# Scores of two heads in the two halves of TensorE's rows, from fp32r high and low parts, in place of one head at a time from three bf16 parts

## The reference, cut to what matters

```python
q = (x @ Wq + bq).reshape(B, S, N_HEAD, HEAD_DIM).transpose(0, 2, 1, 3)
k = (x @ Wk + bk).reshape(B, S, N_HEAD, HEAD_DIM).transpose(0, 2, 1, 3)
...
scores = jnp.einsum('bhqd,bhkd->bhqk', q / math.sqrt(HEAD_DIM), k)
scores = scores + attention_bias
scores = jnp.where(src_mask, -jnp.inf, scores.astype(jnp.float32))
probs = jax.nn.softmax(scores, axis=-1).astype(v.dtype)
ctx = jnp.einsum('bhqk,bhkd->bhqd', probs, v)
```

## Time and profile before

| | before |
|---|---|
| median of three runs | 1060.0 us |
| the profiled execution | 1060.6 us, of which the span of the instructions 1058.7 us |
| PE busy (whole span) | 1006.1 us, 95% |
| DVE, ACT, POOL busy | 840.7 us (79%), 790.2 us (75%), 634.2 us (60%) |
| bytes moved by DMA | 269 MB |

### The profile page before, as it was taken

One profiled execution on the slowest core, in us unless ns is written; L12 is line 12 of the kernel. 1 busy time (PEld: TensorE's weight loads), 2 busy tenths in 40 slices (PEclk: granted clock), 3 DMA queues, 4 the chain that ended last, 5 costly groups with the idle time before them and its releaser, 6 DMA issues.

```text
span 1058.7 us, 19427 instructions
## 1 busy us (share of the span) xinstructions
PE 1006.1 (95%) x6870; PEld 758.3 (72%) x6936; DVE 840.7 (79%) x1966; ACT 790.2 (75%) x1291; POOL 634.2 (60%) x333
## 2 busy tenths in 40 slices
PE   5999999999799999999999999999999799999998
PEld 4789988888565655656666665666666589999997
DVE  6599999998868988989889898998988555555553
ACT  6755577555599899999999999999999344444443
POOL 3565766664246877798787997878877332222110
PEclk9999999999899999999999999999999999999999
DMA  8746788759799999998999989999895131111001
GB/s 234 263 146 222 247 295 301 276 180 378 304 330 398 409 373 358 352 340 322 367 355 340 357 322 362 345 347 343 313 338 199 40 120 60 60 61 40 21 20 40
DMA packets 103249, 269.44 MB, mean 254 GB/s; under 512 B 7522, under 2 KB 63586, under 8 KB 86642
## 3 DMA queue, kind: packets, MB, share of 16 engines
q1 hardware_dynamic: 103154, 268.21, 70.5%
HBM read 217.57 MB, written 50.61 MB: 253 GB/s over the span
## 4 chain that ended last, share of the span: by engine, by line
PE 49%; DVE 12%; DMA 12%; POOL 10%; ACT 8%; issue 7%; SPq 2%; DVEq 0%; ACTq 0%; POOLq 0%
PE psH L540 11%; DMA t_bt<-in_fside_Bx16xSxS 10%; PE psO L540 10%; PE psT L650 9%; POOL t_bt L1423 8%; PE psQ L540 5%; PE psV L663 5%; PE psS L639 4%; ACT t_bt L894 3%; DVE t_x L1026 2%; SPq L255 2%; PE psA L540 2%; ACT t_pt L780 2%; DVE t_bt L1215 2%; PE psX L692 1%
## 5 line engine op out<-in xcount | busy, mean ns | idle before, releaser
L1423 POOL TENSOR_TENSOR t_bt<-t_bt,t_mb 128x1024 f32<-128x1024 f32 x182 | 384.6, 2147 | 89.0 <-DMA t_bt<-in_fside_Bx16xSxS 88.8
L1215 DVE CUSTOM_DVE_ANT_0 t_bt<-psS,t_bt 128x512 f32<-128x512 f32 x512 | 338.2, 684 | 61.1 <-PE psS L639 39.6
L894 ACT ACTIVATE t_bt<-t_bt,t_nm 128x512 f32<-128x512 f32 x512 | 356.6, 732 | 20.4 <-DVE t_nm L1215 20.3
L650 PE MATMUL psT<-t_idf,t_bt 128*128 128x128 f32 x2048 | 308.6, 274 | 5.2 <-issue 2.5
L650 PEld LDWEIGHTS psT<-t_idf,t_bt 128*128 128x128 f32 x2048 | 252.9, 141 | 66.0 <-ACT t_bt L894 12.7
L780 ACT ACTIVATE t_pt<-psT 128x512 f32<-128x512 f32 x317 | 191.2, 603 | 18.9 <-PE psT L650 18.2
L639 PE MATMUL psS<-t_ks,t_qs 128*128 128x512 bf16 x482 | 183.9, 382 | 8.0 <-DVE t_nm L1215 3.7
L1225 DVE COPY t_pt<-psT 128x512 f32<-128x512 f32 x195 | 133.8, 686 | 1.7 <-PE psT L650 1.7
L663 PE MATMUL psV<-t_pt,t_vs 128*17 128x512 f32 x1024 | 134.2, 598 | 0.0
L639 PEld LDWEIGHTS psS<-t_ks,t_qs 128*128 128x128 bf16 x512 | 50.0, 98 | 83.0 <-DVE t_nm L1215 62.8
L1357 POOL TENSOR_SCALAR t_crs<-t_cmv 128x4 f32<-128x4 f32 x8 | 4.2, 519 | 134.8 <-DVE t_cmv L1018 134.8
(11 more groups left out here) (171 smaller groups left out, 2045.1 us busy)
## 6 DMA issues: line engine op xcount, KB each, us to landing
t_bt<-in_fside_Bx16xSxS SPq DMA_DIRECT2D x128, 1024.0 KB, 7.4
sc_qk<-t_parts SPq DMA_DIRECT2D x32, 768.0 KB, 6.6
t_qs<-sc_qk SPq DMA_DIRECT2D x16, 1024.0 KB, 9.8
t_ks<-sc_qk SPq DMA_DIRECT2D x16, 1024.0 KB, 12.2
t_wo_f<-in_L_cond_Wo SPq DMA_DIRECT2D x8, 1024.0 KB, 7.5
sc_qk<-t_parts SPq DMA_DIRECT2D x16, 512.0 KB, 7.4
t_wi_f<-in_L_cond_Wi SPq DMA_DIRECT2D x7, 1024.0 KB, 5.3
sc_v<-t_v SPq DMA_DIRECT2D x8, 544.0 KB, 7.6
```

Of the source, the lines that this page charges most:

```text
L650: ins = e.transpose(psT[turned_bank(n)][:, kk, :], bt[u % NB][:, t, kk * 128:(kk + 1) * 128], idf[:, :])
L894: e.activation(p, p, ACT.Exp, bias=nm[:, n % 16:n % 16 + 1], scale=-1.0).then_inc(a_exp, 1)
L1215: e.tensor_tensor_reduce(bt[u % NB][:, t, :], s, bt[u % NB][:, t, :], -1.0, 3.0e38, ALU.add, ALU.min, nm[:, n % 16:n % 16 + 1]).then_inc(v ...
L1423: e.tensor_tensor(bt[u % NB][:, hs, :], bt[u % NB][:, hs, :], mb[b % 2][:, hs, :], ALU.add).then_inc(g_M, 1)
```

## The change

q and k are no longer split into three bf16 parts but into two fp32r parts, high and low, and the scores are high x high + high x low + low x high: 3 x 16 = 48 rows for a head. Two heads lie in one tile of q and k, one from partition 0 and one from partition 64 (`HALF`), and PE makes their scores with two matmuls, one in each half of its rows. The tiles go by pairs: tiles n and n + 1 are the same 128 query rows of two heads (`place`). A buffer `bt` now holds half of the rows of two heads, and the host lays out the bias to match. PE's `attention` does two tiles in one call: two score matmuls, then the transposes of two older tiles. `LAG` is 5. The fourth bank of `psT` becomes the fourth of `psS`.

ACT writes the high part straight from PSUM (no `qf`), and DVE the low part, as (PSUM + bias) - high; there is no third part, so POOL has no work there. The factor 0.25 goes into Wq. k's products of the first six batches go to `psH` instead of `psQ`. SP stores two pieces for q and two for k (three each before), and loads q and k with two DMAs each, of 48 partitions, 4 heads and 2 KB.

```diff
-TERMS = [(0, 0), (0, 1), (0, 2), (1, 0), (1, 1), (1, 2), (2, 0), (2, 1)]
-NP3 = len(TERMS)
-KR = HD * NP3
+KR = 3 * HD
+HALF = 64
-NB, NP, NS, EARLY, MORE = 5, 8, 3, 5, 21
+NB, NP, EARLY, MORE = 5, 8, 5, 24
-LAG, XLAG, PSTEP, CLAG, SLAG, FIRST = 4, 1, 4, 2, 12, 20
+LAG, XLAG, PSTEP, CLAG, SLAG, FIRST = 5, 1, 4, 2, 12, 20
...
+def place(n):
+    return 2 * (n // 8) + n % 2, n % 8 // 2
+def score_bank(n):
+    return n % 3 if n < MORE else (n - MORE + 3) % 4
...
             def load_qk(n):
...
-                    load(d_q[n % 2], dst[n % 2][:, :, :], sc_qk[b, w, :, :, half, :].rearrange("(h d) i s -> (d i) h s", d=HD))
+                    src = sc_qk[b, w, :, :, half, :].rearrange("(h g d) i s -> g (d i) h s", g=2, d=HD)
+                    for g in range(2):
+                        load(d_q[n % 2], dst[n % 2][HALF * g:HALF * g + KR, :, :], src[g])
...
             def scores(n):
-                P.wait_ge(v_max, n - NS + 1)
-                if not on_pool(u):
+                P.wait_ge(v_max, n + 1 - score_depth(n + 1) + 1)
+                if not on_pool(c):
...
-                    e.matmul(s, idb[:, :], mb[b % 2][:, t, :], start=True, stop=False)
-                e.matmul(s, qs[g % 2][:, h % 8, t * 128:(t + 1) * 128], ks[g % 2][:, h % 8, :], start=on_pool(u), stop=True).then_inc(p_sc, 1)
+                    for i in range(2):
+                        e.matmul(psS[score_bank(n + i)][:, :], idb[:, :], mb[b % 2][:, t, :], start=True, stop=False)
+                for i in range(2):
+                    r = slice(HALF * i, HALF * i + KR)
+                    e.matmul(psS[score_bank(n + i)][:, :], qs[g % 2][r, h % 8 // 2, t * 128:(t + 1) * 128].bitcast(F32R), ks[g % 2][r, h % 8 // 2, :].bitcast(F32R),
+                             start=on_pool(c), stop=True).then_inc(p_sc, 1)
...
             def attention(n):
-                if n == 19:
+                if n % 2:
+                    return
...
-                if 0 <= n - LAG < N:
-                    turn_p(n - LAG)
+                for m in (n - LAG, n - LAG + 1):
+                    if 0 <= m < N:
+                        turn_p(m)
...
-                        e.activation(qf[n][:, mt, :], psQ[mt][:, :], ACT.Identity, bias=bqk[:, n, mt:mt + 1], scale=scale).then_inc(a_qf, 1)
+                        e.activation(parts[n][:, 0, mt, :].bitcast(F32R), qk_bank(b, n, mt)[:, :], ACT.Identity, bias=bqk[:, n, mt:mt + 1]).then_inc(a_qh, 1)
...
-                    copy(parts[n][:, 0, :, :], qf[n][:, :, :], a_p0)
-                    if n:
-                        low(b, 0)
...
-                    rest(b, n)
+                    for mt in range(NK):
+                        yield
+                        P.wait_ge(a_qh, 4 * b + 2 * n + mt + 1)
+                        e.scalar_tensor_tensor(out=parts[n][:, 1, mt, :].bitcast(F32R), in0=qk_bank(b, n, mt)[:, :], scalar=bqk[:, n, mt:mt + 1], in1=parts[n][:, 0, mt, :],
+                                               op0=ALU.add, op1=ALU.subtract).then_inc(v_ql, 1)
...
-            def third(b):
-                for n in range(2):
...
-                    e.tensor_tensor(parts[n][:, 2, :, :], qr[n][:, :, :], parts[n][:, 1, :, :], ALU.subtract).then_inc(g_p2, 1)
```

More of the change, by code:

```diff
@@ L240, in program, with qk_bank @@
             os_.append(sbuf(st, "os1", [128, NT, D]))
+        def qk_bank(b, n, mt):
+            return psH[mt] if n and b < B - 2 else psQ[mt]
         w_chunks, load_w_at, split_w_at, at = {}, {}, {}, 100
@@ L336, in store_part @@
             def store_part(b, n, a):
-                P.wait_ge(g_p2, 2 * b + n + 1)
+                P.wait_ge(v_ql, 4 * b + 2 * n + 2)
                 dst = sc_qk[b, n].rearrange("p i k s -> p i (k s)")
                 src = parts[n][:, :, :, :].rearrange("p c k s -> p c (k s)")
-                g = slice(3 * a, min(3 * a + 3, NP3))
-                k = g.stop - g.start
-                load(d_p[n], dst[:, g, :], src[:, 0:k, :] if n else src[:, a:a + 1, :].broadcast_to([128, k, NK * S]))
+                if n == 0 and a == 0:
+                    load(d_p[n], dst[:, 0:2, :], src[:, 0:1, :].broadcast_to([128, 2, NK * S]))
+                elif n == 0:
+                    load(d_p[n], dst[:, 2:3, :], src[:, 1:2, :])
+                elif a == 0:
+                    load(d_p[n], dst[:, 0:2, :], src[:, 0:2, :])
+                else:
+                    load(d_p[n], dst[:, 2:3, :], src[:, 0:1, :])
             def store_parts(b, n):
-                for a in range(3):
+                for a in range(2):
                     store_part(b, n, a)
@@ L583, in qkv @@
                         P.wait_ge(v_x2Tl, NK * (b + 1))
-                        if n:
-                            P.wait_ge(a_qf, 4 * b + mt + 1)
-                        mm3(psQ[mt][:, :], [([u[:, kk, ms] for u in wsm[w]], [z[:, kk, :] for z in x2T]) for kk in range(NK)], p_q)
+                        if n and b < B - 2:
+                            P.wait_ge(v_hTl, 8 * (b + 2) + NH + mt + 1)
+                        elif n:
+                            P.wait_ge(v_ql, 4 * b + mt + 1)
+                        mm3(qk_bank(b, n, mt)[:, :], [([u[:, kk, ms] for u in wsm[w]], [z[:, kk, :] for z in x2T]) for kk in range(NK)], p_q)
                         yield
@@ L649, in turn_p @@
                 for kk in range(NT):
[L650 removed]
+                    ins = e.transpose(psT[n % 3][:, kk, :], bt[u % NB][:, t, kk * 128:(kk + 1) * 128], idf[:, :])
                 ins.then_inc(p_T, 1)
@@ L825, in turn_x2 @@
                     copy(x2T[0][:, kk, :], psQ[kk][:, :], a_x2Th)
-            def low(b, n):
-                P.wait_ge(v_qr, 2 * b + n + 1)
-                P.wait_ge(g_p2, 2 * b + n - 1)
-                copy(parts[n][:, 1, :, :], qr[n][:, :, :], a_p1)
             def qkv(b):
-                for n, scale in enumerate((0.25, 1.0)):
+                for n in range(2):
                     for mt in range(NK):
@@ L1468, in gpsimd_program @@
             root(rs[1], mv[1], 1e-5, (v_var2, B), g_rs2)
-            for b in (B - 2, B - 1):
-                if b == B - 2:
-                    while at < 4:
-                        attention(at)
-                        at += 1
-                else:
-                    while at < 14:
-                        attention(at)
-                        at += 1
-                third(b)
             while at <= N + LAG - 1:
```

118 lines of the change are left out of this document (51 added, 67 removed).

## The result

The changed kernel takes **1164.95 us** (median of 1160.31 to 1168.89), the kernel before 1061.62: a ratio of 1.097, with a 95% interval from 1.094 to 1.100. It is 10% slower, and 70 us above the range.

What follows compares the result with a forecast made beforehand. The prediction took PE to bound the kernel, with ACT close behind. From 1060.6 us, +18 for attention, -4 for the first stage and -8 for the transition gave 1066.6, stated as 1066 us, range 1024 to 1095.

Steps and rivals of the forecast that it cites:

- DMA: Attention's loads of q and k: three quarters of the bytes, freeing 0.04 of the DMA engines' time; counted as nothing.
- Rival 4: Attention's loads into 48 partitions keep the DMA engines twice as long: +51, 1100 us; chance 0.07.
- (a) to (c): PE's costs in attention: 0.24 us a pair's stream, 0.10 a tiling change, 0.17 a pair for late weight loads.
- rival 1: PE in attention: row halves need no drain, loads hide, ACT becomes the bound: 1032 us; chance 0.33.
- rival 2: PE in attention: the halves' weights load one behind the other, 0.11 us more a pair: 1091 us; chance 0.07.
- rival 3: PE in attention: the two halves' matmuls do not run side by side: +67, 1116 us; chance 0.06.
- it alone decides the sign: Claim that PE's cost per tiling change in attention, taken as 0.10 us, settles whether the kernel gets faster or slower.
- PE bounds the kernel before: Attention before the change: PE sets the tile at 1.005 of the measured 1.037 us, with ACT close behind.
- +18: Attention: PE's costlier score pairs add 0.040 us a tile over some 450 tiles, +18 us.
- First stage -4: Six batches with q, k and v: PE waits less for DVE's low parts of h, -4 us.
- Transition -8: About 260 to 313 us: POOL's third-part subtractions and ACT's copies go, -8 us, between -3 and -10.
- The banks and the lag: Attention: four psS and three psT banks and a lag of five keep PE about three tiles ahead: nothing.

Runs made afterwards that it cites:

- the spread run: Changed kernel with its four loads of q and k issued behind tiles 4, 10, 16 and 22 of each 32, not all behind tile 4: 1142.68 us.
- the run through the whole array: Kernel with 64 rows a head, k's load 14 tiles behind q's, each score matmul over all 128 partitions instead of row halves: 1057.67 us.
- loads apart: Changed kernel with 64 rows a head and one load each for q and k, k's issued 14 tiles behind q's: 1065.83 us.

## Why the prediction was wrong, point by point

**DMA: the step that failed.** "a quarter less frees 0.04. As DMA is not the bound, I count nothing." This priced the loads by their bytes, at the rate of loads into 128 partitions. They pass at 175 GB/s instead of 367, so three quarters of the bytes take 1.57 MB / 175 = 9.0 us per 32 tiles instead of 2.1 / 347 = 6.0. The difference between the changed kernel and the one without reloads is 97 us. One load over all partitions gives 86 of them back although it carries a third more bytes, and 96 against two loads of the same bytes. The term that stood at nothing was worth some 97 us.

**Rival 4 was this mechanism, at 0.07 and at 1100 us.** It gave the loads twice their time, 0.32 instead of 0.16 of the engines, and nothing else. In truth they took 1.5 times their old time: by its own sum 0.24 instead of 0.16, 1.03 x 1.037 = 1.068 a tile, some 14 us and not 51. What it left out is what stands behind them: the bias loads come from the same queue, beside slow packets they are slow as well (505 instead of 341 ns in the spread run), for 9 us at a stretch too little bias lands for POOL, and PE, made to wait, runs at a lower clock afterwards. How much of the 97 us each of these is, no run separates. The sign it gave, DVE and POOL waiting for loads, is what the waits show. Its chance was too low for a form of load that no row had shown: "No row has such a load" was a reason to fear it. The Trainium skill (SBUF — State Buffer, Door 1: The DMA port swizzle) was named there and stood for a chance of 0.07; the estimates from its figures held to within some 8%.

**PE, (a) to (c): right.** The sum was 17.14 us for 16 tiles, 1.07 a tile. Without reloads PE is full at 1.061, and where no context group lies between, the run through the whole array saves 0.047 a tile by going without the changes and their late loads, where the sum had 0.055. Rivals 1, 2 and 3 are out by the pair's rows: 0.53 and 0.42 us where rival 1 said 0.43 and 0.24, and 3 ns between the two matmuls. But "it alone decides the sign" was wrong: the loads did. And the prediction compared row halves only with row halves that do not overlap (rival 3); two matmuls through the whole array, which it did not price, are cheaper by 6 to 8 us in the run.

**PE bounds the kernel before: half right.** For the kernels with fp32r pairs it holds (449.75 of 450 us busy; a lighter PE brings 9 to 10 us). For the kernel before, a lighter PE with a heavier POOL brought nothing. PE (435 of 450 us), ACT (427) and the DMA engines (0.95) stood too close together there to name one. Which of them holds it was not separated.

**Attention without the loads.** +18 was said. From tile 20 to 511 the run without reloads needs 525.3 us, that with loads apart 522.3, against 509.5: +16 and +13. Right in size.

**First stage -4: right**, -3.8. PE is busy for the whole batch, where it had holes before.

**Transition -8: too large**, -5.3, inside its bounds of -3 to -10. PE's wait for the normalisation fell, and ACT's copies near 300 us are gone, but there is a wait for DVE's low parts of 2.2, where I had put the cost at 0.3. PE's weight loads from 258 to 304 us:

```profile
PEld psQ L592 <- DVE t_x L1049: 2.4, 1, 2.4
...
PEld psQ L556 <- DVE t_parts L1156: 2.2, 2, 1.1
```

The first was 6.8.

**The banks and the lag: right**, nothing by themselves; the run with loads apart has them and is where PE's sum puts it.

## What to carry to other kernels

A load's price depends on which partitions it lands in, so a change that makes tiles narrower in partitions (48 or 64 of 128) must be priced by a row of such a load or, without one, be forecast as slow; here, filling the other partitions with a redundant term was 86 us cheaper than leaving them out. A queue that is nearly full is charged for a slow transfer twice, once for its own time and once for what stands behind it: here the loads themselves took some 3 us more in 32 tiles, and the 32 tiles over 6 us more than with fast loads apart (40.4 and 34.0). Two small matmuls side by side, between operations on the whole array, pay for the change of tiling on both sides, so one compares them with two through the whole array, not with each other's stream.

## What the runs showed of the hardware that I had not expected

- The rate of a load by its span: 48 partitions 162 to 175 GB/s (rows of 8 and 2 KB), 64 partitions 203 to 211 (1 and 2 KB), 128 partitions 367 to 405 (1, 2 and 8 KB), and all with the DMA engines shown as full (1.01 to 1.14). The busy share does not tell a slow load from a fast one; the GB/s beside it does.
- Two loads into the two halves, issued one behind the other, do not add up: 211 GB/s together.
- One operation of DVE from SBUF to SBUF, of 4 elements a partition, ended only when POOL paused, and not behind one of POOL's operations: 8.92 us behind the rest of seven additions, 0.17 where POOL had pauses. The 5.44 in the earlier trace rows had already shown a wait behind one operation of POOL. DVE's copies from PSUM ran beside the same additions at 0.69.
- A wait for the loads also cost TensorE's clock. In the changed kernel, by stretch as above:

```profile
542.00:546.00 4.00, 1.59 (x12) 0.95 (x10) 0.00 (x0) 1.07 (x2) 2.35 (x2) 0.97 1.02 416
546.00:550.00 4.00, 2.54 (x12) 0.87 (x12) 3.82 (x10) 1.93 (x3) 4.00 (x3) 0.50 1.01 419
```

PE stood still for 2.4 of 4 us, and in the next 4 us the granted clock was 0.50, the level of 1.2 GHz instead of 2.4. Over the stage it was 0.93 on the mean; in the run without reloads, where PE waited once for 0.2 us, 1.00.
